# Cross attention scores: two query heads in one 128-column stationary operand

## The chip, the cores and the metric

The kernel runs on one core of a Trainium2 chip. The metric is device time in microseconds (us) of one execution. The engines are named as the profile names them: PE is TensorE's matmul stream, PEld its weight loads, DVE is VectorE, ACT is ScalarE, POOL is GpSimd, SP is SyncE, which issues the DMAs. In a matmul the stationary operand is loaded into TensorE's array first (a weight load, LDWEIGHTS) and the moving operand then streams through it; the columns of the stationary operand become the partitions of the output.

## The reference

One layer of a perceiver: cross attention of 64 latents to the first 64 positions of a context (a causal mask over 64 queries hides the rest), self attention, and a feed-forward block with routed low-rank experts. What matters here is the cross attention, with 16 batches, 32 query heads, 8 key and value heads of width 128:

```python
queries = rope((q @ Wq.T).reshape(B, Sq, 32, 128).transpose(0, 2, 1, 3))
keys    = rope((k @ Wk.T).reshape(B, Skv, 8, 128).transpose(0, 2, 1, 3))
keys = jnp.repeat(keys, 4, axis=1)                 # 4 query heads share a key head
scores = jnp.einsum('bhqd,bhkd->bhqk', queries, keys) * 128 ** -0.5
scores = jnp.where(causal[None, None], scores, finfo.min)
attn = jax.nn.softmax(scores, axis=-1)
ctx = jnp.einsum('bhqk,bhkd->bhqd', attn, values)
x = x + ctx.transpose(0, 2, 1, 3).reshape(B, Sq, 4096) @ Wd.T
```

## The kernel before

Every engine has its own instruction stream, written out by hand, and semaphores tie them together; within an engine the order is the order of the code. The keys and values of all 8 key heads are computed first and spilled to memory (up to about 118 us). Then `head(g, n, ...)` on TensorE works through key heads g = 0 to 6 (0 and 6 written out, 1 to 5 as a loop), and a last stretch of code does key head 7. In the text a "head" is such a key head with its four query heads.

In one head TensorE alternates between two heads' work: the scores, transposes, probability-value products and output products of head g, and the query projection of head n = g + 1, which is cut into `product` calls (line 1559). All products with weights use FP32R operands, split into a high and a low part; scores (line 1618), transposes (line 1625) and probability-value products (`pv_x`, line 1638) are plain FP32. `out_x` (line 1651) multiplies the context by the output weights.

The scores of a head come in four chunks of four batches each, `scores_x(g, 0)` to `scores_x(g, 3)`. They are issued as two groups: chunks 0 and 1 at the head's start, chunks 2 and 3 after the first two products. A chunk fills one PSUM bank, `sc[:, c, :]`: partitions 0 to 63 have the 64 queries of one query head (r = 0), partitions 64 to 127 those of the next (r = 1), and eight blocks of 64 keys lie side by side. The stationary operand is the rotated queries `qr[128, batch, query head, 64 positions]`, the moving one the rotated keys `kr` of 64 positions. The two matmuls of r = 0 and r = 1 stand next to each other in the stream and use the left and the right half of the array's columns.

After a chunk, its last matmul raises `scored`. VectorE adds the mask (`mask_max`, line 1195) and takes the maximum (line 1197), GpSimd subtracts it (line 517), ScalarE exponentiates (line 793), VectorE sums and inverts (lines 1210 and 1212), GpSimd normalises (line 522); TensorE transposes the result (line 1625), ScalarE copies it (line 797), and `pv_x` uses it. ScalarE and VectorE split its output into a high and a low part (lines 801 and 1216). Between these, the same three engines rotate the next queries (lines 493, 499, 672, 673, 1067) and split weights (line 511).

In the feed-forward block `hidden` (line 1970) is a plain FP32 matmul on the whole array, with 128 stationary and 137 moving columns; it stands between output products of the self attention (line 1920) and others, which are FP32R on the whole array.

Of the kernel before, what the change touches and what calls it, by code (L numbers as in the profile page):

```python
# [12 lines left out]
B, S, D = 16, 64, 512  # L13
# [48 lines left out]
def build(nc, x, ctxT, w_k, w_v, w_q, w_d, w_s, w_o, w_b, w_ag, w_eb, consts, bias_cols, bias_rows, b_thr,  # L62
          kscr, vscr, out):
    es = ExitStack()
    with es:
# [3 lines left out]
        def sb(stack, name, shape, dt=F32):  # L69
            return stack.enter_context(nc.sbuf_tensor(name, shape, dt))  # L70
# [33 lines left out]
        qr = sb(xs, "qr", [P, B, REP, S])  # L104
        kr = sb(xs, "kr", [P, B, S])
# [95 lines left out]
        def pb(name):  # L201
            return es.enter_context(nc.psum_tensor(name, [P, 2, 512], F32))
        pj, sc, tp, pv = pb("pj"), pb("sc"), pb("tp"), pb("pv")
# [1296 lines left out]
        def _(pe):  # L1500
# [106 lines left out]
            def scores_x(g, j, held=False):  # L1607
                h, c = j // 2, j % 2
                if h == 1:
                    pe.wait_ge(masked, 4 * g + j - 1)  # L1610
                else:
                    pe.wait_ge(x_done, XD0 + 8 * g - 3 + (0 if held else c))
                for b in range(4):
                    bb = 8 * h + 4 * c + b
                    for hp in range(2):
                        blk = (b // 2 * 2 + hp) * 2 + b % 2
                        for r in range(2):
                            last = pe.matmul(sc[64 * r:64 * r + 64, c, blk * S:(blk + 1) * S],  # L1618
                                             qr[:, bb, 2 * hp + r, :], kr[:, bb, :], start=True, stop=True)
                last.then_inc(scored, 1)  # L1620

            def p_transposes(g, j):
# [33 lines left out]
            def head(g, n, more, first=False):  # L1656
# [8 lines left out]
                pe.wait_ge(rope, Q0 + 6 if first else ri(m, 0))  # L1665
                pe.wait_ge(s_kr, 16 * (g + 1))
                scores_x(g, 0)
                scores_x(g, 1)
                pe.wait_ge(wlo, 2 * m + 1)
                if not first:  # L1670
# [5 lines left out]
                if first:  # L1676
                    pe.wait_ge(rope, ri(m, 0))
                scores_x(g, 2)
                scores_x(g, 3)
                pe.wait_ge(wlo, 2 * m + 2)  # L1680
# [261 lines left out]
            for m in range(N_SS // 2):  # L1942
                n = 2 * m
                v, c = n // SCH, n % SCH
# [77 lines left out]
            for i in range(NT):  # L2022
                pe.wait_ge(hw_done, i + 1)
                last = pe.transpose(sc[:, i // 4, (i % 4) * P:(i % 4 + 1) * P], hw[:, i, :], ident)
# [79 lines left out]
```

## Time and profile before

| | |
|---|---|
| time, median of 3 runs | 727.95 us (727.66 to 728.04) |
| profiled execution, its own time | 727.08 us |
| its span, first to last instruction | 725.3 us |
| mean granted TensorE clock | 0.998 |
| PE busy | 707.9 us (98%) |
| PEld, DVE, ACT, POOL busy | 564.9, 514.3, 373.2, 486.7 us |

The profile shows one execution. Matmuls are pipelined and overlap weight loads and one another, so busy PE time is not time at its peak. Each line of the trace gives an engine, the line of the kernel, the operation, its output and inputs, and durations; "idle before" is how long the engine had been idle ahead of it, with what released it.

### The profile page before, as it was taken

The page shows a single profiled execution, that of the slowest core. Times are in us where ns is not written, and L with a number is a line of the kernel's source. Part 1 is how long each engine was busy: PE and PEld are TensorE (multiplying, and loading weights), DVE is VectorE, ACT ScalarE, POOL GpSimd, SP SyncE. Part 2 cuts the span into 40 slices and gives each one's busy share as a digit, 9 for nine tenths or more (in the row PEclk, how much of TensorE's full clock was granted, in tenths as well). Part 3 has the DMA queues.
Part 4 walks back from the last instruction along what each step waited for, and adds up shares of the span by engine and source line. Part 5 has one row for each costly group of instructions (what it writes and reads, how often), then busy time and mean ns, then how long its engine had stood idle before and what let it go on. Part 6 is the DMA issues. An engine that isn't in the chain of part 4 may idle for free.

```text
span 725.3 us, 12895 instructions
## 1 busy us (share of the span) xinstructions
PE 707.9 (98%) x4848; PEld 564.9 (78%) x4848; DVE 514.3 (71%) x811; ACT 373.2 (51%) x559; POOL 486.7 (67%) x366
## 2 busy tenths in 40 slices
PE   9999999799999999999999999998999999998997
PEld 7788887577778777778778778776777888887886
DVE  5756878857857767757757757757657888898735
ACT  5456664644643743653653564554236677664220
POOL 1898555777867867867867867846324799984630
PEclk9999999999999999999999999999999999999999
DMA  8554513131310311301311212200200100020003
GB/s 284 201 173 135 165 54 115 45 131 45 117 43 31 106 37 43 101 29 43 101 41 45 88 43 73 74 15 5 99 0 2 44 31 30 2 58 32 15 1 116
DMA packets 25561, 51.09 MB, mean 70 GB/s; under 512 B 2352, under 2 KB 10672, under 8 KB 25520
## 3 DMA queue, kind: packets, MB, share of 16 engines
q1 hardware_dynamic: 25520, 50.53, 20.8%
q8 instruction: 27, 0.44, 0.2%
q14 instruction: 14, 0.11, 0.1%
HBM read 40.04 MB, written 10.49 MB: 70 GB/s over the span
## 4 chain that ended last, share of the span: by engine, by line
PE 84%; DVE 7%; POOL 4%; ACT 2%; issue 1%; DMA 1%; SPq 0%; DVEq 0%; POOLq 0%
PE pj L1559 11%; PE sc L1651 10%; PE pj L1651 9%; PE pj L1750 8%; PE tp L1559 8%; PE pv L1545 5%; PE pv L1638 4%; PE tp L1651 3%; PE sc L1618 3%; PE pj L1920 3%; PE tp L1533 2%; PE sc L1800 2%; PE tp L1813 2%; PE pv L1824 2%; PE pj L1533 2%; PE tp L1625 2%
## 5 line engine op out<-in xcount | busy, mean ns | idle before, releaser
L493 POOL TENSOR_TENSOR sw<-sw,cst 128x512 f32<-128x512 f32 x72 | 101.0, 1403 | 37.9 <-ACT sw L673 37.7
L517 POOL TENSOR_TENSOR sm<-sm,mx 128x512 f32<-128x512 f32 x64 | 72.1, 1133 | 45.4 <-DVE mx L1197 26.9
L511 POOL TENSOR_TENSOR w<-raw,w 128x896 fp32r<-128x896 f32 x28 | 60.9, 2197 | 34.7 <-ACT w L658 34.7
L499 POOL TENSOR_TENSOR qr<-t,sw 128x512 f32<-128x512 f32 x54 | 73.4, 1359 | 7.8
L522 POOL TENSOR_TENSOR sm<-sm,rz 128x512 f32<-128x512 f32 x64 | 66.0, 1045 | 18.2 <-DVE rz L1212 18.2
L1559 PE MATMUL tp<-x,w 128*128 128x512 f32 x288 | 76.1, 400 | 1.4 <-ACT sw L673 1.4
L793 ACT ACTIVATE sm<-sm 128x512 f32<-128x512 f32 x64 | 40.4, 633 | 69.9 <-POOL sm L517 69.9
L1750 PE MATMUL pj<-xh,ws 128*128 128x512 f32 x192 | 64.3, 401 | 0.2 <-ACT kb L881 0.2
L1559 PEld LDWEIGHTS tp<-x,w 128*128 128x128 f32 x288 | 52.0, 188 | 11.8 <-ACT sw L673 1.7
L658 ACT ACTIVATE w<-raw 128x1792 fp32r<-128x1792 f32 x15 | 25.6, 1707 | 59.8 <-DVE raw L1089 59.8
L1216 DVE TENSOR_TENSOR cl<-pv,ch 128x1024 fp32r<-128x1024 f32 x32 | 39.1, 1222 | 22.7 <-ACT ch L801 22.7
L1559 PE MATMUL pj<-x,w 128*128 128x512 f32 x192 | 51.5, 404 | 0.6 <-ACT pc L711 0.6
L1559 PE MATMUL pj<-xt,w 128*128 128x512 f32 x192 | 51.1, 404 | 0.2 <-DVE cq L1120 0.2
L1210 DVE TENSOR_REDUCE zs<-sm 128x8 f32<-128x512 f32 x64 | 42.8, 668 | 6.2 <-ACT sm L793 5.9
L801 ACT ACTIVATE ch<-pv 128x1024 fp32r<-128x1024 f32 x32 | 32.9, 1028 | 25.2 <-PE pv L1638 24.9
L1559 PEld LDWEIGHTS pj<-xt,w 128*128 128x128 f32 x192 | 34.4, 188 | 13.6 <-DVE cq L1120 4.9
L1651 PE MATMUL sc<-wdh,ch 128*128 128x512 f32 x108 | 43.0, 398 | 0.6 <-DVE cl L1216 0.6
L1559 PEld LDWEIGHTS pj<-x,w 128*128 128x128 f32 x192 | 34.3, 188 | 10.5 <-DVE t L1067 1.7
L1651 PE MATMUL sc<-wdh,cl 128*128 128x512 f32 x108 | 42.2, 391 | 0.0
L672 ACT ACTIVATE sw<-tp 64x512 f32<-64x512 f32 x36 | 21.5, 597 | 40.1 <-DVE t L1067 26.4
L1750 PEld LDWEIGHTS pj<-xh,ws 128*128 128x128 f32 x192 | 36.0, 188 | 7.7 <-ACT kb L881 0.6
L1651 PE MATMUL sc<-wdl,ch 128*128 128x512 f32 x108 | 42.1, 389 | 0.0
(277 smaller groups left out, 1860.9 us busy)
## 6 DMA issues: line engine op xcount, KB each, us to landing
rawd<-in_w_d SPq DMA_DIRECT2D x16, 512.0 KB, 3.3
raw<-in_w_q SPq DMA_DIRECT2D x15, 512.0 KB, 3.3
kscr<-sm SPq DMA_DIRECT2D x16, 256.0 KB, 2.1
vscr<-sm SPq DMA_DIRECT2D x16, 256.0 KB, 2.6
kr<-kscr SPq DMA_DIRECT2D x8, 512.0 KB, 3.2
vv<-vscr SPq DMA_DIRECT2D x16, 256.0 KB, 2.6
raw<-in_w_k SPq DMA_DIRECT2D x4, 512.0 KB, 5.9
cT<-in_ctxT SPq DMA_DIRECT2D x4, 512.0 KB, 6.7
```

Of the source, the lines that this page charges most:

```text
L493: pool.tensor_tensor(bs(sw[par][:, :]), bs(sw[par][:, :]), rep(cst[:, C_SIN:C_SIN + S], HB), ALU.mult).then_inc(sin_done, 1)
L499: pool.tensor_tensor(o, bs(t1[par][:, :]), bs(sw[par][:, :]), ALU.add).then_inc(rope, 1)
L511: pool.tensor_tensor(w7[p][:, 1, c], raw[:, 1:8, :].rearrange("p n c -> p (n c)")[:, c], w7[p][:, 0, c].bitcast(F32), ALU.subtract).then_i ...
L517: pool.tensor_tensor(s3, s3, per_group(mx[:, c, :], 8), ALU.subtract).then_inc(subbed, 1)
L522: pool.tensor_tensor(s3, s3, per_group(rz[:, c, :], 8), ALU.mult).then_inc(normed, 1)
L793: act.activation(sm4[c][:, :], sm4[c][:, :], ACT.Exp, scale=scale).then_inc(exped, 1)
L1210: dve.tensor_reduce(zs[:, c, :], bs(sm4[c][:, :]), AXX, ALU.add).then_inc(summed, 1)
L1216: dve.tensor_tensor(by_bank(cl, c % 2), pv4, by_bank(ch, c % 2).bitcast(F32), ALU.subtract).then_inc(pv_lo, 1)
L1545: last = pe.matmul(pv[:, vi % 2, :], a[:, k, tok], wv[gg][:, r, k, :], start=(k == 0 and part == 0), stop=(k == KT - 1 and part == 2))
L1559: last = pe.matmul(bank, a, r, start=(start and k == 0 and part == 0), stop=(stop and k == 1 and part == 2), skip_group_check=True)
L1651: last = pe.matmul(banks[j], a[:, c, at + r, :], w[:, r, :], start=(r == 0 and part == 0), stop=(r == REP - 1 and part == 2))
L1750: last = pe.matmul(pj[:, k % 2, :], ws[t][:, part // 2, i, c], (xl if part == 1 else xh)[:, i, tok], start=(m == 0), stop=(m == 3 * KT - 1))
```

## The change

The two matmuls of neighbouring query heads become one, whose stationary operand is both heads' 64 query columns, which lie next to each other in `qr`. Its 128 output partitions are those that the two matmuls wrote together. Everything else stays.

```diff
                     bb = 8 * h + 4 * c + b
                     for hp in range(2):
                         blk = (b // 2 * 2 + hp) * 2 + b % 2
-                        for r in range(2):
-                            last = pe.matmul(sc[64 * r:64 * r + 64, c, blk * S:(blk + 1) * S],
-                                             qr[:, bb, 2 * hp + r, :], kr[:, bb, :], start=True, stop=True)
+                        last = pe.matmul(sc[:, c, blk * S:(blk + 1) * S],
+                                         qr[:, bb, 2 * hp:2 * hp + 2, :].rearrange("p r s -> p (r s)"), kr[:, bb, :],
+                                         start=True, stop=True)
                 last.then_inc(scored, 1)
```

## Rows read from the trace of the kernel before

**Rows 1.** The page: busy time, the clock in 40 slices, the chain by engine.

```profile
PE 707.9 (98%) x4848; PEld 564.9 (78%) x4848; DVE 514.3 (71%) x811; ACT 373.2 (51%) x559; POOL 486.7 (67%) x366
...
PEclk9999999999999999999999999999999999999999
...
PE 84%; DVE 7%; POOL 4%; ACT 2%; issue 1%; DMA 1%; SPq 0%; DVEq 0%; POOLq 0%
```

**Rows 2.** Windows: length, busy PE, PEld, DVE, ACT, POOL (instructions), clock, DMA.

```profile
118.00:163.00 45.00, 39.24 (x286) 29.45 (x287) 33.48 (x46) 22.17 (x32) 31.53 (x22) 1.00 0.31 110
163.00:207.00 44.00, 44.00 (x318) 34.51 (x315) 33.43 (x46) 22.35 (x32) 34.99 (x26) 1.00 0.21 73
```

**Rows 3.** Line 1618: duration in ns (min/median/max), and its idle time before.

```profile
L1618 PEld LDWEIGHTS sc<-kr,qr x1024: 132/138/138, 118.8 to 496.4; 128*64 128x64 f32 x171
...
  issue: 5.3, 15
```

**Rows 4.** The chain that ended last, pieces of heads 1 to 6.

```profile
179.10 2.02 PE sc L1618 x64
...
253.71 2.72 PE sc L1651 x12
...
442.56 2.02 PE sc L1618 x64
```

**Rows 5.** Timeline of one score group and its neighbours (start, length).

```profile
284.11 0.39 PE L1651 MATMUL tp<-wdl,ch 128*128 128x512 f32 x1
284.43 0.31 PEld L1618 LDWEIGHTS sc<-kr,qr 128*64 128x64 f32 x7 [0.35 <-issue]
...
285.63 0.69 DVE L1195 TENSOR_TENSOR sm<-sc,cst 128x512 f32<-128x512 f32 x1 [0.40 <-PE sc L1618]
...
286.44 0.30 PEld L1559 LDWEIGHTS pj<-x,w 128*128 128x128 f32 x2
```

**Rows 6.** Groups of instructions by line and form: plain FP32 on the whole array.

```profile
L1970 PE MATMUL sc<-wag,xf 128*128 128x137 f32 x64 | 8.0, 279 | 0.0
L1970 PEld LDWEIGHTS sc<-wag,xf 128*128 128x128 f32 x64 | 8.0, 189 | 0.2
...
L1504 PEld LDWEIGHTS sc<-cst,cq 128*128 128x128 f32 x32 | 3.7, 140 | 0.5
```

**Rows 7.** Timeline from line 1920 to line 1970 and back.

```profile
680.22 0.64 PE L1970 MATMUL sc<-wag,xf 128*128 128x137 f32 x4
...
681.87 0.19 PEld L1970 LDWEIGHTS sc<-wag,xf 128*128 128x128 f32 x1
681.99 0.19 PEld L1920 LDWEIGHTS pj<-woh,ah 128*128 128x128 f32 x1
```

**Rows 8.** The chain in head 0.

```profile
138.74 6.11 POOL w L511 x2
...
152.00 2.97 PE sc L1651 x12
```

**Rows 9.** Timeline of PE in head 0, where it waited.

```profile
131.21 1.65 PE L1559 MATMUL tp<-x,w 128*128 128x512 f32 x6 [1.42 <-ACT sw L673]
...
135.60 1.14 PE L1638 MATMUL pv<-pt,vv 64*128 64x256 f32 x8 [1.14 <-ACT pt L797]
```

**Rows 10.** The chain at the entry to head 7.

```profile
491.26 0.61 DVE sm L1195
...
501.63 0.48 ACT pt L797
```

**Rows 11.** Timeline of PE there.

```profile
499.60 0.66 PE L1625 MATMUL tp<-cst,sm 128*128 128x128 f32 x4
...
504.44 0.96 PE L1638 MATMUL pv<-pt,vv 64*128 64x256 f32 x4 [2.78 <-DVE cl L1216]
```

**Rows 12.** Windows there: length, PE busy (matmuls), clock, DMA.

```profile
503.00:509.00 6.00, 4.57 (x19) 0.72 0.26 67
505.00:507.00 2.00, 2.00 (x11) 0.50 0.00 0
```

## The prediction

> **What bounds the kernel now.** The page comes first: TensorE (PE) is busy for 98% of the span, its clock is at the top level of 2.4 GHz in every slice of the page, and 84% of the chain that ended last is PE [rows 1]. Because a share is an average over stages, I next cut the cross attention, the only stage that the change touches, into stretches of one head. From 163 to 207 us PE is busy in all 44.00 us, while VectorE, ScalarE and GpSimd have 9 us or more to spare, and the equal heads below say the same up to 442; in the stretch ahead of it, which holds head 0, PE has 39.24 of 45 us [rows 2]. Head 0 and the entry to head 7 come separately below. So in heads 1 to 6 whatever PE gains or loses goes into the time in full.
>
> The view of line 1618 shows what the scores are made of: 1,024 weight loads of 64 columns, each with a matmul [rows 3]. The code issues 512 matmuls (32 chunks of 16), so an FP32 matmul leaves two records of each kind. In the chain a group of two chunks stands as one piece of 64 matmuls and 2.02 us, and the piece at 442.56 comes 263.46 us after that at 179.10, five heads of 52.69 us [rows 4]. In the timeline of one group, the last matmul ahead of it starts at 284.11, the first score weights only at 284.43, and the first weights of the next product at 286.44; its second load, which goes out when its first matmul starts, at 286.44 + 0.30 - 0.19 = 286.55 (two loads span 0.30, and one of 128 columns is 0.19) [rows 5, 6]. A matmul of 512 columns in an undisturbed stream takes 2.72 / 12 = 0.227 us [rows 4]. So a group occupies PE for 286.55 - 284.11 - 0.227 = 2.21 us. This is more than its piece, since on both sides the next load does not start behind the last matmul but after a pause: PEld stands idle for 0.35 us for "issue" ahead of the scores, 15 times [rows 3, 5]. Where the array is used whole, no such pause appears.
>
> **The change part by part.** Per chunk, 16 matmuls with 64 weight columns become 8 with 128, so 512 become 256 and their records 512 of each kind. Output rows, banks, the single increment of `scored` per chunk and all waits stay; no other engine and no DMA gets or loses an instruction.
>
> *What it removes: concurrency.* Now 32 loads of each half run in about the time of one half's: 64 records in 2.02 us are 32 pairs of 0.063 us, first load included, though each load of 64 columns is recorded at 0.138 us. Two heads per pair then cost 0.063 us per record. After the change one record of 128 columns does the same work, and the question is how fast a whole array is reloaded when each matmul moves only 64 columns.
>
> *What it adds: loads of full width.* No row has a full-width FP32 load with so short a matmul, so I bound it. At 286.44 two loads of 128 columns follow each other with nothing to stream: 0.30 - 0.19 = 0.11 us apart [rows 5, 6]. From above, the plain FP32 matmuls of line 1970, with full-width loads and 137 moving columns, stand 64 in 8.0 us, 0.125 us each, and four in a row start (0.64 - 0.28) / 3 = 0.12 us apart [rows 6, 7]; part of that is streaming. From below, a load of 128 columns is recorded at 0.188 and one of 64 at 0.138 [rows 3, 6]: if all else in a load is a fixed delay, 64 columns are 0.050 and 128 are 0.100 us. The row nearest in kind is the bare pair of loads, and I take 0.110 us per record. The matmul itself is shorter than the present pair's 0.063 and hides behind the next load. The Trainium skill ("TensorE: Matmul & The Clock Gate", section "LDWEIGHTS (loading the stationary operand)") has load time grow with the columns at 1.2 per ns, so 0.107 us for 128; as an estimate from the Trainium skill a group would take 3.42 us, and the trace's 0.11 agrees.
>
> *What it gives back: the pauses.* Lines 1920 and 1970 go from FP32R to plain FP32 and back on the whole array: the last load of line 1970 starts at 681.87 and the first of line 1920 at 681.99, one record later, with no pause [rows 7]. So I let the pauses go. The first load of a group then hides behind the preceding 0.227 us matmul, and 31 loads and the next product's first one stay exposed: 32 x 0.110 = 3.52 us per group against 2.21, or +1.31. The Trainium skill ("TensorEngine Tiling (Array Packing)", section "Key Properties") says that a change of tiling mode drains the engine, which agrees with the pauses of rows 5 and would have them vanish here.
>
> *Heads 1 to 6.* Two groups each, 12 in all, on a PE that never waits: 12 x 1.31 = 15.7 us. The mask on VectorE (line 1195) already waits for scores there (0.40 us in the group shown [rows 5]); a chunk comes at most 1.31 us later per group, and behind that instruction queue the maximum, GpSimd's subtraction and pieces of the next query products. But PE, which needs those results, is later by the same 1.31 or more, so I cost this at nothing; without that cover it could not exceed the shift itself.
>
> *Head 0.* Its chain does not run through PE until 152.00 us: before that it goes through VectorE, ScalarE and GpSimd, with 6.11 us in two GpSimd subtractions (line 511) [rows 8]. PE waits 1.42 us at 131.21 and 1.14 at 135.60, both for ScalarE copies [rows 9]. Two groups would bring 2.62 us, and these two waits alone, 2.56, take it up. Cost 0; if the cover fails, up to 2.62.
>
> *Entry to head 7.* VectorE leads the chain from 491.26, and ends it with the release of a PE that has waited 2.78 us [rows 10, 11]. There ScalarE's copy of the second transposed probabilities runs at 501.63, of transposes that PE did from 499.60 to 500.26 [rows 10, 11]. Two groups later, 2.62 us, these end at 502.88, so the copy and all behind it are 1.25 us later, and PE's wait shrinks to 2.78 + 1.25 - 2.62 = 1.4 us. Right after the present wait the clock falls: over 503 to 509 it is 0.72 in the mean, with 0.50 from 505 to 507 [rows 12]. That is 6 x 0.28 / 0.50 = 3.4 us at 1.2 GHz, some 1.7 us lost. In head 0 the waits of 1.42 and 1.14 us went by with the clock at 1.00 [rows 2, 9]. So I expect the fall not to come, and the entry to cost 1.25 - 1.7 = -0.45 us; bounds -1.7 (nothing on the chain) and +2.62 (all of it, and the fall as well).
>
> *Sum.* 15.7 + 0 - 0.45 = +15.3 us on the profiled execution's 727.08 (span 725.3 and 1.8 around it), 742.4. The median of the runs is 727.95, 0.87 higher, which makes 743.2.
>
> **Rivals.** *Faster: the full-width load is no limit.* A transpose loads 128 columns too, recorded at 0.140 us, not 0.188 [rows 6], so quick loads exist. If the period stayed at 0.063, a group would be 2.02 us without pauses, and 12 x (2.02 - 2.21) = -2.3 us give 725.7. It decides below 2.21 / 32 = 0.069 us; around that the time would be unchanged. Against it: the non-transposed loads of rows 5 and 7 are 0.11 and more apart. 5 in 100, and 3 in 100 for no change, which also holds the case that PE's shift is absorbed somewhere I don't see.
>
> *Loads don't overlap matmuls.* Then a record takes 0.11 + 0.063 = 0.173 us, a group 5.54, and 12 x 3.33 = 40 us make 768 or more. Against it, line 1970 has 0.12 us where load and matmul in turn would be over 0.17 [rows 7]. 4 in 100. The Trainium skill ("TensorE: Matmul & The Clock Gate", section "What overlaps and what doesn't") would have this: weights load beside a running matmul only in another row group, and here all rows are used; the trace disagrees.
>
> *The clock falls in the groups.* The groups' matmuls would stand further apart than any others in these heads. If each of 16 groups brought a fall like that of rows 12, 16 x 1.7 = 27 us more: 770. For it, a clock that has fallen after a wait of 2.78 us; against it, a clock of 1.00 through head 0 with its several waits. 6 in 100.
>
> **How the numbers follow.** My case has 82 in 100. Its low end takes 0.100 per record, 12 x 0.99 = 11.9, and -1.7 at head 7: 738. Its high end takes 0.125, 12 x 1.79 = 21.5, and 2.62 each for heads 0 and 7: 755. That range holds 8 in 10. Faster by over 0.2%, about what a measurement here can tell: 0.05; within it 0.03; slower 0.92.
>
> **What would show it.** Right: 512 records of each kind at line 1618, loads of about 0.188 us, the "issue" pauses gone, score pieces of 3.5 us, equal pieces 52.7 + 2.6 = 55.3 us apart per head, head 0 with less PE waiting and the same length, and no fall of the clock after 504 us plus the shift. Wrong: pieces of 2 us (quick loads), of 5 us (no overlap), a clock below 1.00 in heads 1 to 6, or other engines' waits ahead of PE there.

## The result and the profile after

The changed kernel takes 742.1 us (median of 4 runs, 741.75 to 743.24), the kernel before beside it 727.8 us (724.73 to 728.04). The ratio is 1.0203, 95% interval 1.0185 to 1.0221: slower by 14.3 us. The forecast was 743.2 us, range 738 to 755. The profiled execution took 741.75 us with a span of 740.0.

The page after, busy time as in [rows 1]:

```profile
PE 726.3 (98%) x4336; PEld 591.5 (80%) x4336; DVE 516.5 (70%) x811; ACT 374.1 (51%) x559; POOL 483.9 (65%) x366
```

PE has 512 matmul records fewer and is busy 18.4 us longer; the other engines have as many instructions as before, and their busy times differ by less than 3 us. The mean granted clock of this execution is 1.000, and PE's share of the chain that ended last is 87%, where it was 84%. The score line (now 1617), as in [rows 3]:

```profile
L1617 PEld LDWEIGHTS sc<-kr,qr x512: 187/192/192, 118.3 to 514.0; 128*128 128x128 f32 x171
```

Half the records, loads of 192 ns in place of 138, and no idle time ahead of them any more. One group in the timeline, as in [rows 5]:

```profile
288.74 0.39 PE L1651 MATMUL tp<-wdl,ch 128*128 128x512 f32 x1
288.75 0.41 PEld L1617 LDWEIGHTS sc<-kr,qr 128*128 128x128 f32 x2
...
292.32 0.19 PEld L1617 LDWEIGHTS sc<-kr,qr 128*128 128x128 f32 x1
...
292.43 0.30 PEld L1559 LDWEIGHTS pj<-x,w 128*128 128x128 f32 x2
```

The first score load starts 0.01 us after the start of the preceding matmul (before, 0.32 us), and the product's first load 0.11 us after the last score load: both pauses are gone. The product's second load is at 292.43 + 0.30 - 0.19 = 292.54, so a group occupies 292.54 - 288.74 - 0.227 = 3.57 us, 32 records of 0.112 us, against 2.21 before. The chain, as in [rows 4]:

```profile
178.81 3.52 PE sc L1617 x32
...
454.63 3.52 PE sc L1617 x32
```

The same pieces are now 275.82 us apart over five heads, 55.16 us each, 2.47 more than before. The windows of [rows 2] (length, busy PE, PEld, DVE, ACT, POOL, clock, DMA):

```profile
118.00:163.00 45.00, 41.53 (x223) 32.68 (x221) 33.47 (x47) 22.16 (x32) 31.77 (x22) 1.00 0.32 108
163.00:207.00 44.00, 44.00 (x240) 36.12 (x239) 31.50 (x43) 22.57 (x32) 33.59 (x26) 1.00 0.22 73
```

Head 0 holds 2.3 us more PE busy time in the same 45 us, and heads 1 to 6 stay full. The place of [rows 12] is behind the wait at the entry to head 7, which ends at 520.73 here; there the clock stays at 1.00 (length, busy PE, clock, DMA):

```profile
519.00:525.00 6.00, 4.44 (x25) 1.00 0.17 48
```

PE's waits in head 0 and at the entry to head 7, as in [rows 9, 11]:

```profile
130.95 1.66 PE L1559 MATMUL tp<-x,w 128*128 128x512 f32 x6 [0.57 <-ACT sw L673]
135.34 1.13 PE L1638 MATMUL pv<-pt,vv 64*128 64x256 f32 x8 [1.16 <-ACT pt L797]
...
520.73 1.14 PE L1638 MATMUL pv<-pt,vv 64*128 64x256 f32 x8 [1.56 <-DVE cl L1216]
```

### The profile page after: what moved, and what is told of

Same layout as the page of the kernel before. It is cut to its first block, busy times and chain, and to the rows that moved or that the text cites. A ratio compares the mean times of both kernels' runs of the same rounds, so it can differ in the third digit from the quotient of the medians.

```text
span 740.0 us, 11871 instructions
## 1 busy us (share of the span) xinstructions
PE 726.3 (98%) x4336; PEld 591.5 (80%) x4336; DVE 516.5 (70%) x811; ACT 374.1 (51%) x559; POOL 483.9 (65%) x366
## 4 chain that ended last, share of the span: by engine, by line
PE 87%; DVE 5%; POOL 4%; ACT 2%; issue 1%; DMA 1%; SPq 0%; DVEq 0%; POOLq 0%
PE pj L1559 11%; PE sc L1651 10%; PE pj L1651 10%; PE pj L1750 8%; PE tp L1559 8%; PE sc L1617 7%; PE pv L1545 5%; PE pv L1638 4%; PE tp L1651 4%; PE pj L1920 3%; PE tp L1533 2%; PE sc L1800 2%; PE tp L1813 2%; PE pv L1824 2%; PE pj L1533 2%; PE tp L1625 2%
## 5 line engine op out<-in xcount | busy, mean ns | idle before, releaser
L499 POOL TENSOR_TENSOR qr<-t,sw 128x512 f32<-128x512 f32 x54 | 71.7, 1328 | 7.7
L1617 PEld LDWEIGHTS sc<-kr,qr 128*128 128x128 f32 x512 | 59.6, 192 | 1.2
L1617 PE MATMUL sc<-kr,qr 128*128 128x64 f32 x512 | 58.9, 273 | 0.0
```

Of the source, the lines that this page charges most:

```text
L499: pool.tensor_tensor(o, bs(t1[par][:, :]), bs(sw[par][:, :]), ALU.add).then_inc(rope, 1)
L1617: last = pe.matmul(sc[:, c, blk * S:(blk + 1) * S], qr[:, bb, 2 * hp:2 * hp + 2, :].rearrange("p r s -> p (r s)"), kr[:, bb, :], start=Tru ...
```

## The experiments

All times are medians, and ratios are to the kernel before on the same chip. Its median beside the first four kernels below is 727.7 us, beside the next two (the orders two by two and four by four) 726.7, and beside the last three (parts of the heads) 727.8. In the code, `<two heads>` stands for the stationary operand of the change, and `...` for arguments that stay.

### The load sets the period: more moving columns, fewer stationary ones

The changed kernel with twice the moving columns (the added products are of no use, and the scores are not the reference's):

```diff
-last = pe.matmul(sc[:, c, blk * S:(blk + 1) * S], <two heads>, kr[:, bb, :], ...)
+at = min(blk, 6) * S
+last = pe.matmul(sc[:, c, at:at + 2 * S], <two heads>,
+                 kr[:, min(bb, B - 2):min(bb, B - 2) + 2, :].rearrange("p b s -> p (b s)"), ...)
```

> The changed kernel, but each score matmul streams the keys of two neighbouring batches, 128 columns instead of 64, and the second batch's 64 columns are overwritten or left as they fall, so the scores are not the reference's. Theory (the period of a record is that of its full-width load, 0.112 us): twice the columns hide behind the load, at most as in line 1970 (0.118 with 137 columns), a group of 3.58 to 3.78 us, 742 to 745. Rival (the period is load plus matmul, or the matmul sets it): 0.053 us more per record, 1.7 us per group, 12 groups 20 us, about 762.

743.2 us, ratio 1.0222 (1.0199 to 1.0245): that of the changed kernel within the interval, and far from the rival's 762. In the other direction, 96 stationary columns:

```diff
-last = pe.matmul(sc[:, c, blk * S:(blk + 1) * S], <two heads>, kr[:, bb, :], ...)
+last = pe.matmul(sc[0:96, c, blk * S:(blk + 1) * S], <two heads>[:, 0:96], kr[:, bb, :], ...)
```

> The changed kernel, but with 96 of the 128 stationary columns, so half of every second head's queries get no scores. Theory (the period is the time to load the columns): 0.112 x 96 / 128 = 0.084 us per record, a group of 2.69 us instead of 3.58, 12 groups 10.7 us less, about 732 (730 to 735). Rival (a fixed cost per full-array record, whatever its width): no change against the changed kernel, 742.

732.3 us, ratio 1.0069 (1.0044 to 1.0094), 9.8 below the changed kernel. A piece of the chain in each, first that with twice the moving columns:

```profile
290.72 3.57 PE sc L1618 x32
```

```profile
286.24 2.69 PE sc L1617 x32
```

Against the 3.52 us of the changed kernel's piece, twice the streaming costs 0.05 us per group; a quarter of the load's columns less takes 3.52 - 2.69 = 0.83 us off, 24% of the piece. So the period is the load's, and neither a fixed cost per record nor load and matmul in turn.

### The pauses belong to the passage between halves and whole array

The kernel before, with the change in the second half of each chunk only:

```diff
 for hp in range(2):
     blk = (b // 2 * 2 + hp) * 2 + b % 2
+    if b >= 2:
+        last = pe.matmul(sc[:, c, blk * S:(blk + 1) * S], <two heads>, kr[:, bb, :], ...)
+        continue
     for r in range(2):
```

> Per chunk the first two batches with the two halves, as before, and the last two with the whole array, as after; so each group changes between halves and whole array four times, where the kernel before does it twice and the changed one never. Matmul time of a group: 16 pairs of records of 0.058 and 16 records of 0.112 = 2.72 us. Theory (each passage into the halves and out of them costs a pause, 0.29 us for both): 2.72 + 2 x 0.29 = 3.31 us per group against 2.21 before, 12 groups 13 us, less some 1.5 of used-up waits: about 739 (737 to 741). Rival (the pauses belong to the change between FP32R and FP32 or to semaphores at the group's ends, and are there once): 2.72 + 0.29 = 3.01, 736; or none at all, 733.

740.3 us, ratio 1.0188 (1.0163 to 1.0212), as the theory has it and above its rivals' 736 and 733. One group in the chain:

```profile
289.12 0.62 PE sc L1623 x16
289.74 1.03 PE sc L1618 x8
290.77 0.61 PE sc L1623 x16
```

A fourth piece of 1.03 us follows. The price of a record in the halves is read from the kernel before, where the loads of the group of [rows 5] are

```profile
284.43 1.95 PEld L1618 LDWEIGHTS sc<-kr,qr 128*64 128x64 f32 x64 [0.35 <-issue]
```

so that the last pair starts 1.95 - 0.14 = 1.81 us after the first, 0.058 us for each of 31 pairs. There is no FP32R and no wait inside a chunk, yet the eight whole-array records take 1.03 us and not 8 x 0.112 = 0.90, and the sixteen of the halves 0.62 and not 8 x 0.058 = 0.46: each passage adds its 0.13 to 0.16 us in the middle as well.

### What the halves gave: concurrency, and how near the neighbour has to be

The kernel before with its 512 matmuls in another order, nothing else:

```diff
-for b in range(4):
-    for hp in range(2):
-        for r in range(2):
+for r in range(2):
+    for b in range(4):
+        for hp in range(2):
             last = pe.matmul(sc[64 * r:64 * r + 64, c, blk * S:(blk + 1) * S],
                              qr[:, bb, 2 * hp + r, :], kr[:, bb, :], start=True, stop=True)
```

(The lines that compute `bb` and `blk`, not shown, move with their loops.)

> The kernel before with the same 512 score matmuls in another order: within a chunk first the eight of the left half of the columns, then the eight of the right half. Theory (what the change removes is that a load and matmul of one half run beside those of the other, and that needs neighbours in different halves): the 64 records of a group then take 0.058 us one after the other instead of two by two, 32 x 0.058 = 1.86 us more per group, a group of 4.07 us; over 12 groups 22 us, less some 1.5 us of small waits that a later PE uses up, so about 749 (745 to 753). Rival (the halves overlap in whatever order they are issued): about 728.

743.8 us, ratio 1.0231 (1.0206 to 1.0257). The direction is the theory's, and the rival, no loss, is excluded; but the size is below the expected 745 to 753. The piece of the chain is 3.34 us:

```profile
291.38 3.34 PE sc L1618 x64
```

That is 1.32 more than 2.02, not 1.86; 0.54 us are missing, or 0.18 at each of the three boundaries between the sides, three records of 0.058. The starts of the loads in the trace show it: within a side they are 0.058 us apart, and at each boundary three loads of one side start within 0.005 us of three of the other. Two more orders were run on that: runs of two matmuls on a side (`for b: for r: for hp`), and runs of four (`for b pair: for r: for b: for hp`).

> The kernel before with its score matmuls two by two: per batch two of the left half, then two of the right, runs of four records on a side. In the half-by-half order a boundary between the sides saved about 0.18 us, three records of 0.058, as if the right half started when three records of the left were left. Theory (the two halves overlap if the other half's next load is at most about three records away): four records on a side with three overlapped at each of 15 boundaries reach the floor of the alternating order, 2.2 to 2.4 us per group, 728 to 730. Rival (only a direct neighbour in the other half overlaps): one record at each boundary, 3.71 + 0.35 - 15 x 0.058 = 3.2 us per group, about 738.

> The same with runs of four matmuls, eight records, on a side. Theory (three records overlap at each of 7 boundaries): 3.71 + 0.35 - 7 x 0.175 = 2.83 us per group, 0.62 more than before, 12 groups 7.4 us: about 735. Rival (only a direct neighbour): 3.71 + 0.35 - 7 x 0.058 = 3.65 us, about 743. Second rival (any order within a chunk overlaps but for the last boundary): about 728.

727.1 us, ratio 1.0004 (0.9985 to 1.0023), and 736.5 us, ratio 1.0115 (1.0087 to 1.0144), both the theory's and not the rivals' 738, 743 and 728, though the first lies 0.9 below its range (the kernel before beside it took 726.7) and the second 1.5 above its "about 735". Their pieces, first two by two, then four by four:

```profile
285.61 2.06 PE sc L1618 x64
```

```profile
288.00 2.62 PE sc L1619 x64
```

So at each change of side about three records run beside three of the other side, and what is left of a longer run goes one after the other; runs of four records lose next to nothing. Why the reach is three, no run shows. What the change gave up is this concurrency: one order of the old matmuls that lets most of it go costs as much as the change.

### Where the loss lies: head 0, head 7, heads 1 to 6

The change in one part of the heads alone, by a condition on `g`, here for head 0 (`g == NKV - 1` for head 7; `not isinstance(g, int) or 0 < g < NKV - 1` for heads 1 to 6):

```diff
+    if isinstance(g, int) and g == 0:
+        last = pe.matmul(sc[:, c, blk * S:(blk + 1) * S], <two heads>, kr[:, bb, :], ...)
+        continue
     for r in range(2):
```

> The change in head 0 alone, two groups. Theory (head 0 is led by VectorE, ScalarE and GpSimd, and PE's waits take the 2.7 us up): no change, within 0.5 us of the kernel before. Rival (PE's time is on the path there too): 2.7 us more, about 730.5.

727.4 us, ratio 0.9996 (0.9982 to 1.0011): no change, and the rival's 2.7 us lie outside the interval.

> The change in head 7 alone, two groups. Theory (the chain there gets 1.25 us longer, PE's wait falls from 2.78 to about 1.4 us, and the clock no longer falls, which gives back 1.7 us): 0.5 us less than before, within 1 us of it either way, and a clock of 1.00 from 500 to 515 us in its trace. Rival (the clock falls all the same): 1.25 us more, about 729. Second rival (all of it on the path): 2.7 us more.

727.9 us, ratio 1.0004 (0.9991 to 1.0018): no change either; the first rival's 1.25 us lie at the interval's upper end, so the trace has to tell. It has PE's wait near the theory's 1.4 and the clock (windows: length, PE busy, clock, DMA) at the theory's 1.00:

```profile
506.38 1.13 PE L1643 MATMUL pv<-pt,vv 64*128 64x256 f32 x8 [1.56 <-DVE cl L1216]
```

```profile
500.00:515.00 15.00, 13.44 (x76) 1.00 0.23 71
```

> The change in heads 1 to 6 alone, 12 groups. Theory (PE never waits there, so that each group's 1.37 us goes into the time, less about 0.25 us per head of small waits): 12 x 1.37 - 1.5 = 14.9 us more, about 742.7, all of the loss of the changed kernel and a little more. Rival (a part of the loss is in heads 0 and 7): 737 to 740.

743.2 us, ratio 1.0201 (1.0173 to 1.0229): the whole loss. With head 7 as before, its wait (2.74 us, up to 520.27) and the fall of the clock (0.81 in the mean over 518 to 527 us) are there again.

## Why the prediction was right

- *The period of a whole-array record.* Taken as 0.110 us from two bare loads, measured 0.112. That it is the load's is shown from both sides, by 128 moving and by 96 stationary columns. The upper bound from line 1970 (0.12 with 137 moving columns) lies above it; that its columns take longer to stream than 128 take to load fits the 0.112 of 128 moving columns, but no run separates it. Per record the traces have 0.058 us with 64 stationary columns, 2.69 / 32 = 0.084 with 96 and 0.112 with 128; at 64 the moving columns are 64 too, so that figure alone could not tell load from streaming. The Trainium skill ("TensorE: Matmul & The Clock Gate", section "LDWEIGHTS (loading the stationary operand)") has the load grow with the columns, and the traces agree.
- *The pauses.* Let go in the sum, and gone in the trace; that the passage between the two uses of the array makes them is shown by the kernel that does both. The runs give the price, 2.21 - 32 x 0.058 = 0.35 us for in and out, which includes the exposed first load. The Trainium skill ("TensorEngine Tiling (Array Packing)", section "Key Properties") names such a drain, without a price.
- *Heads 1 to 6.* 12 groups in full: predicted +1.31 each and 15.7, measured +1.36 and 2 x 1.36 = 2.72 per head, of which 2.47 arrived. The step "a PE that never waits" was off by 0.25 us per head. The view of waits for PE's loads has, before and from 163 to 464 us,

```profile
PEld pj L1559 <- ACT u L711: 1.9, 6, 0.4
```

  and this line is missing after. Those short waits lay under the modelled ends of matmuls, so PE looked busy through them, and a later PE used them up. In the chain of one head it is the product that waited for that copy which gets shorter, first before and then after,

```profile
294.96 1.57 PE pj L1559 x6
```

```profile
302.26 1.38 PE pj L1559 x6
```

  and the product ahead of it goes from 1.46 to 1.39 us: 0.26 together. The two errors, +0.05 per group and -0.25 per head, are +0.6 and -1.5 us over the six heads, and cancel only in part: 6 x 2.47 = 14.8 us arrived instead of 15.7.
- *Head 0.* No change, as forecast, shown by the run of head 0 alone. But the waits that took it up were partly others than the two that the forecast added up, so that their sum of 2.56 us against 2.62 was right by luck: that at 131.21 fell from 1.42 to 0.57 us and those of 0.77 and 0.61 ahead of it, not among the rows of the sum, went altogether, while that at 135.60, counted at 1.14, stayed at 1.16.
- *Entry to head 7.* Forecast -0.45 us from a chain 1.25 longer and 1.7 given back by the clock, PE's wait 1.4. Measured: a wait of 1.56, a clock of 1.00, and 0.0004 of the time (-0.7 to +1.3 us). In the trace of head 7 alone the wait ends 506.38 - 489.70 = 16.68 us after the start of the last matmul ahead of the first score group, before 504.44 - 489.27 = 15.17, so the chain is 1.5 us longer; from the wait's end to the next `pv_x` it is 513.99 - 506.38 = 7.61 us where it was 513.66 - 504.44 = 9.22, so the clock gives 1.6 back. The forecast took this gift as certain, but it depends on the execution: of the 23 of the kernel before beside this experiment, 6 have a mean granted clock of 1.000 (one fall as in [rows 12] makes it 0.998), and their mean is 726.0 us; of the 12 with head 7 changed, 10 have 1.000, and their mean is 727.9. At equal clock head 7 thus costs about 1.9 us (1.2 to 2.6). The near zero is this cost against a fall that mostly stays away. That the clock was at the top level in every slice of the page was also too strong: a digit 9 is 90% or more, and the 1.7 us of the fall are 9% of a slice of 18.1 us.
- *Rivals.* Quick full-width loads (725.7), loads and matmuls in turn (768) and a clock that falls in the groups (770) are excluded by the period of 0.112 and a clock of 1.00 throughout heads 1 to 6. The 0.140 us on which the first rested was the length of a record and not a period: in the chain of the kernel before, eight of those transposes (line 1504, at 527.19) take 0.87 us, 0.11 each. Twice the moving columns add 0.05 us to a group and not 32 times their streaming. The section "What overlaps and what doesn't" of the Trainium skill's page "TensorE: Matmul & The Clock Gate" has loads wait for matmuls that use the same rows, and this contradicts it again.

## What to carry to other kernels

A matmul with few moving columns cost its weight load here, so count the columns that are loaded per microsecond and not matmuls: two halves that load and stream side by side beat one whole-width matmul (0.058 against 0.112 us for the same work), even after paying the pauses of going in and out. Such concurrency depends on the order of issue: here about three records ran beside those of the other half. And a change is priced by stage: the same 2.7 us per head were worth 2.5 where PE set the time, nothing in head 0, where PE waited for others, and in head 7 some 1.5 to 1.9 us, which a clock that mostly stopped falling hid. So look at the granted clock of every execution, and compare at equal clock: with it at 1.000 in all of them, the changed kernel (two executions, 742.1 us) is 16 us behind the kernel before (726.0), not 14.3.

## What the runs showed that was not expected

The reach of the overlap between the halves: orders with runs of 2 records on a side, of 4, of 8 and of 16 have pieces of 2.02, 2.06, 2.62 and 3.34 us. And a wait's length alone does not tell whether the clock falls. With 96 columns PE waited 1.70 us at the entry to head 7, hardly more than the 1.56 us that left the clock at 1.00, and the clock fell (0.76 in the mean over 509 to 516 us). In the order two by two PE waited longer there, and the clock stayed up (windows: length, PE busy, clock, DMA):

```profile
505.73 1.13 PE L1638 MATMUL pv<-pt,vv 64*128 64x256 f32 x8 [2.62 <-DVE cl L1216]
```

```profile
500.00:515.00 15.00, 12.38 (x70) 1.00 0.25 70
```

In that execution it fell instead behind a wait of 1.83 us at line 1920 (0.94 in the mean over 650 to 680 us); the kernel before has a wait of 1.8 us at that line too, and a clock of 1.00 over 660 to 726 us. The prediction let the fall of one trace stand for all executions and took a wait of 1.4 us as safe because others of that length had been; that it came out so for most of them was in part luck. What decides it in one execution stays open.
